# Two experts in one tile: slots of 64 rows, half-width matmuls, the second half's weights copied by ScalarE

## The chip, the cores and the metric

The kernel runs on one core of one Trainium2 chip. The metric is device time in microseconds (us) of one execution, the median of several.

## What is computed

A transformer block in fp32: causal attention with 16 heads on 4 x 512 tokens of width 512, between layer norms, and then a mixture of experts. Only the second part matters here. Each of 2048 tokens goes to 8 of 64 experts, each a gated layer of width 128, and the 8 results are added with their weights. A shared expert is added for every token.

```python
E = 64; K = 8; D = 512; F = 128; FS = 128
logits = xt @ router_w.T
probs = jax.nn.softmax(logits.astype(jnp.float32), axis=-1)
top_w, top_i = jax.lax.top_k(probs, K)
top_w = top_w / jnp.sum(top_w, axis=-1, keepdims=True)
comb = comb.at[jnp.arange(T)[:, None], top_i].set(top_w)
def step(acc, ws):
    wg_e, wu_e, wd_e, we = ws
    h = jax.nn.silu(xt @ wg_e.T) * (xt @ wu_e.T) @ wd_e.T
    return (acc + we[:, None] * h, None)
routed, _ = jax.lax.scan(step, jnp.zeros_like(xt), (Wg, Wu, Wd, comb.T))
```

## The kernel before

The program of each engine is written out by hand, with semaphores between them. After attention (to about 430 us) and the router, VectorE (DVE) and TensorE (PE) sort the 2048 x 8 pairs of token and expert by expert into slots; each expert's rows are padded to a multiple of 128, so a tile of 128 slots belongs to one expert. `place_rows` and `tile_rows` (PE) and lines L1180 to L1252 (DVE) work out the first slot of each expert (`below`, `steps`), the expert of each tile (`col_i`), the slot of the ring in which its weights lie (`ring_i`), the number of expert weights that a tile needs loaded (`weights_i`), the tile after which a ring slot is free (`ends_i`) and the number of loop bodies (`pairs_i`). The table of tokens, 128 rows by `HIGH` = 192 tiles, is filled by 128 pairs of one-hot matrices (DVE, L1243 and L1244) and matmuls (PE, L910), beside the shared expert's 16 tiles (L853, L863, L869).

Then the expert loop runs over 6q + 1 tiles in bodies of six (`DEEP`). For a tile t:

- GpSimd (POOL) gathers 128 rows of activations and router weights by index (L458), up to six tiles ahead, and after `down` adds 128 result rows to one of three sum tables in memory (L464). It is the only engine that issues these.
- PE: `turn_rows` transposes the rows (L940, four of 128x128), `up` multiplies them with the gate and up weights (L956, four matmuls of 256 moving columns), `turn_hidden` transposes the gated product (L962) and `down` multiplies it with the down weights (L967, one of 512 columns). In the loop the order is `down(t-1)`, `turn_rows(t+2)`, `turn_hidden(t)`, `up(t+1)`.
- ScalarE (ACT): `silu(t)` (L659), then `turned(t+2)`, which waits that the weights of the tile are loaded (`s_ready`, the index from `weights_i`, L651) and copies the turned rows out of PSUM (L654).
- DVE: `hide(t)` (L1277), `take_y(t-1)` (L1284, L1285), `take_hidden(t)` (L1289), `weight(t+1)` (L1271, one column of the gathered row, found by a register load from `col_i`) and `stage_gather` (L1262).
- SyncE (SP) loads each expert's 768 KB into a ring of eight (L353) when the last tile that uses the slot is through (`s_dn`).

In attention, `weigh` (L779) multiplies with 32 columns of weights into four groups of 32 PSUM partitions, and `score` (L729) uses 32 rows in four groups. After the loop three tables are added, normalised and written out.

## Time and profile before

| | us |
|---|---|
| median of 3 runs | 1173.48 (1173.42 to 1176.66) |
| profiled execution | 1176.2 |
| its span, first to last instruction | 1174.3 |
| PE busy | 1080.3 |
| DVE busy | 683.6 |
| POOL busy | 630.4 |
| ACT busy | 483.4 |

The span is divided by engine. PE is busy nearly all the time; the other engines are busy for about half of it. Busy time tells how much work an engine has, not who waits: for that the groups of instructions, the waits and the order of time in a short stretch are read. Times in rows are us, durations of one instruction ns where so marked. A group "x1264" counts records; an fp32 matmul has two. POOL's `DMA_INDIRECT` is the time in which it writes out a gather or scatter, not that of the transfer.

### The profile page before, as it was taken

The page shows a single profiled execution, that of the slowest core. Times are in us where ns is not written, and L with a number is a line of the kernel's source. Part 1 is how long each engine was busy: PE and PEld are TensorE (multiplying, and loading weights), DVE is VectorE, ACT ScalarE, POOL GpSimd, SP SyncE. Part 2 cuts the span into 40 slices and gives each one's busy share as a digit, 9 for nine tenths or more (in the row PEclk, how much of TensorE's full clock was granted, in tenths as well). Part 3 has the DMA queues.
Part 4 walks back from the last instruction along what each step waited for, and adds up shares of the span by engine and source line. Part 5 has one row for each costly group of instructions (what it writes and reads, how often), then busy time and mean ns, then how long its engine had stood idle before and what let it go on. Part 6 is the DMA issues. An engine that isn't in the chain of part 4 may idle for free.

```text
span 1174.3 us, 24363 instructions
## 1 busy us (share of the span) xinstructions
PE 1080.3 (92%) x6281; PEld 726.1 (62%) x6282; DVE 683.6 (58%) x2349; ACT 483.4 (41%) x1357; POOL 630.4 (54%) x648
## 2 busy tenths in 40 slices
PE   6999899999999979988879999999999999999973
PEld 3555566555656546555547777777777777767631
DVE  5666566556666668868845444455444444545447
ACT  2666566656666644433212222222222222222223
POOL 3533333333333313321148788888888888888724
PEclk9999999999999999989979999999999999999987
DMA  8700000000000042100259999999999999997796
GB/s 315 287 2 1 3 1 1 2 2 1 1 2 2 1 187 91 63 19 19 72 177 212 222 198 252 248 234 240 260 232 250 243 229 277 272 226 148 110 334 240
DMA packets 66279, 166.71 MB, mean 142 GB/s; under 512 B 15379, under 2 KB 17171, under 8 KB 66081
## 3 DMA queue, kind: packets, MB, share of 16 engines
q0 software_dynamic: 38496, 83.95, 32.6%
q1 hardware_dynamic: 27712, 81.88, 19.7%
q8 instruction: 38, 0.62, 0.2%
q14 instruction: 33, 0.26, 0.1%
HBM read 119.85 MB, written 62.65 MB: 155 GB/s over the span
## 4 chain that ended last, share of the span: by engine, by line
PE 71%; DMA 12%; DVE 6%; issue 4%; ACT 2%; POOL 2%; POOLq 0%; DVEq 0%; SPq 0%; ACTq 0%
PE ps L956 15%; PE ps L700 15%; DMA sum_rows<-x_t,idx 8%; PE ps L967 8%; PE ps L759 6%; PE ps L817 4%; PE ps L729 4%; PE ps L940 4%; PE ps L779 4%; DMA x_t<-x_rows,idx 3%; PE ps L853 3%; PE ps L714 2%; PE ps L869 1%; PE ps L833 1%; POOL x_t L458 1%
## 5 line engine op out<-in xcount | busy, mean ns | idle before, releaser
L956 PE MATMUL ps<-big,work 128*128 x1264 | 300.5, 381 | 0.0
L464 POOL DMA_INDIRECT sum_rows<-x_t,idx x157 | 250.0, 1592 | 52.3 <-issue 40.2
L956 PEld LDWEIGHTS ps<-big,work 128*128 128x128 f32 x1264 | 229.0, 191 | 24.9
L458 POOL DMA_INDIRECT x_t<-x_rows,idx x159 | 166.2, 1045 | 63.5 <-issue 28.1
L700 PE MATMUL ps<-big 128*128 128x384 f32 x512 | 181.5, 499 | 2.1 <-ACT big L533 1.7
L384 POOL TENSOR_TENSOR work<-qkv_all,rope_sb 128x256 f32<-128x256 f32 x64 | 46.7, 729 | 245.2 <-ACT qkv_all L538 245.2
L654 ACT ACTIVATE work<-ps 128x512 f32<-128x512 f32 x159 | 95.0, 597 | 192.6 <-PE ps L940 131.6
L967 PE MATMUL ps<-big,work 128*128 x314 | 161.2, 595 | 1.8 <-issue 1.6
L940 PEld LDWEIGHTS ps<-ident_sb,x_t 128*128 128x128 f32 x636 | 78.7, 142 | 101.6 <-issue 71.0
L1061 DVE CUSTOM_DVE_ANT_0 ps<-ps,mask_sb 128x128 f32<-128x128 f32 (+3 forms) x256 | 120.6, 512 | 23.8 <-PE ps L729 23.0
L557 ACT ACTIVATE work<-ps,neg_max 128x128 f32<-128x128 f32 (+3 forms) x256 | 132.5, 528 | 3.3 <-DVE neg_max L1061 2.4
L700 PEld LDWEIGHTS ps<-big 128*128 128x128 f32 x512 | 94.8, 195 | 57.3 <-issue 4.6
L1277 DVE SCALAR_TENSOR_TENSOR work<-work,small,ps 128x128 f32<-128x128 f32 x157 | 54.5, 347 | 124.7 <-ACT work L659 97.1
L659 ACT ACTIVATE work<-ps 128x128 f32<-128x128 f32 x157 | 43.6, 278 | 196.4 <-PE ps L956 145.6
L563 ACT ACTIVATE x_t<-ps 128x128 f32<-128x128 f32 (+2 forms) x192 | 77.0, 436 | 90.6 <-PE ps L759 90.6
L940 PE MATMUL ps<-ident_sb,x_t 128*128 128x128 f32 x636 | 97.3, 276 | 14.2 <-DMA x_t<-x_rows,idx 12.5
L759 PE MATMUL ps<-ident_sb,work 128*128 128x128 f32 x640 | 98.5, 284 | 9.7 <-issue 6.6
L1285 DVE TENSOR_SCALAR x_t<-ps 128x512 f32<-128x512 f32 x157 | 106.9, 681 | 0.0
L759 PEld LDWEIGHTS ps<-ident_sb,work 128*128 128x128 f32 x640 | 68.8, 141 | 46.7 <-issue 35.7
L1082 DVE TENSOR_TENSOR attn_t<-ps,work 128x128 f32 (+1 forms) x64 | 18.7, 292 | 111.0 <-PE ps L779 111.0
L1271 DVE TENSOR_SCALAR small<-x_t 128x1 f32 x158 | 24.3, 154 | 76.1 <-issue 72.3
L967 PEld LDWEIGHTS ps<-big,work 128*128 128x128 f32 x314 | 58.9, 190 | 12.9 <-issue 5.2
(177 smaller groups left out, 1459.9 us busy)
## 6 DMA issues: line engine op xcount, KB each, us to landing
big<-experts SPq DMA_DIRECT2D x65, 768.0 KB, 14.5
sum_rows<-x_t POOLq DMA_DIRECT2D x4, 2048.0 KB
big<-sum_rows SPq DMA_DIRECT2D x8, 768.0 KB, 9.5
x_rows<-work SPq DMA_DIRECT2D x16, 256.0 KB, 2.0
sum_rows<-attn_t POOLq DMA_DIRECT2D x2, 2048.0 KB
out<-x_sb SPq DMA_DIRECT2D x16, 256.0 KB, 5.2
x_sb<-x SPq DMA_DIRECT2D x3, 1024.0 KB, 10.2
x_t<-sum_rows SPq DMA_DIRECT2D x4, 768.0 KB, 13.1
```

Of the source, the lines that this page charges most:

```text
L458: pool.indirect_dma_start(rows[:, q, :], None, x2_rows, bass.IndirectOffsetOnAxis(ap=idx[:, q, 0:1], axis=0), bounds_check=last_row, oob_i ...
L464: pool.indirect_dma_start(all_sums, bass.IndirectOffsetOnAxis(ap=idx[:, q, 1:2], axis=0), y_sb[:, q, :], None, bounds_check=last_sum, oob_ ...
L557: act.activation(probs[:, h, 0:n], s_bank[h][:, 0:n], ACT.Exp, bias=neg_max[:, h:h + 1], scale=-1.0, accum_out=den[:, h:h + 1]).then_inc(s ...
L563: act.activation(probs_t[:, i % 2, h, 0:qt + 1, :], pt_bank[h % 2].rearrange("p (k n) -> p k n", k=TB)[:, 0:qt + 1, :], ACT.Copy).then_inc ...
L654: act.activation(rows_t[:, p, :, :], ps[:, p, :].rearrange("p (c n) -> p c n", c=DC), ACT.Copy).then_inc(s_xg, 1)
L700: mm = pe.matmul(bank[:, 0:QKV], x_t[:, c, bass.ts(t, P)], wqkv_sb[:, c, g % G, :], start=(c == 0), stop=(c == DC - 1))
L759: mm = pe.transpose(pt_bank[h % 2][:, bass.ts(c, P)], probs[:, h, bass.ts(c, P)], ident_sb[:, :])
L940: mm = pe.transpose(ps[:, p, bass.ts(c, P)], rows[:, q, bass.ts(c, P)], ident_sb[:, :])
L956: mm = pe.matmul(ps[:, 2 + p, 0:GATEUP], rows_t[:, p, c, :], w_ring[:, slot, c * GATEUP:(c + 1) * GATEUP], start=(c == 0), stop=(c == DC - 1))
L967: pe.matmul(ps[:, 5 + p, :], hidden_t[:, p, :], w_ring[:, slot, DC * GATEUP:WCOLS], start=True, stop=True).then_inc(s_dn, 1)
L1061: dve.tensor_tensor_reduce(sc, sc, mask_sb[:, S - n:S], -SCALE, 3.0e38, ALU.add, ALU.min, neg_max[:, h:h + 1]).then_inc(s_masked, 1)
L1285: dve.tensor_scalar(y_sb[:, q, :], ps[:, 5 + q % 2, :], 1.0, None, ALU.mult).then_inc(s_y, 1)
```

## The change

Slots are counted in units of `GRAIN` = 64: each expert's rows are padded to a multiple of 64, and a tile of 128 slots has two halves that may belong to two experts. `HIGH` becomes 162. `up` and `down` are issued as two matmuls each, one per half: 64 columns of weights (the activations) into PSUM partitions 0 to 63 or 64 to 127. The moving operand of the first half is read from the ring at an address from a register, that of the second from a fixed place, `wb_up` and `wb_down` (two buffers each, in what was attention's `qkv_all`). ACT copies it there for every tile, `copy_up` 128x1024 and `copy_down` 128x512, also where both halves have the same expert. The row's weight is picked by a comparison of the 64 router weights with the half's expert (`expert_p`) and a sum. The tables are worked out for both halves. Left out below are declarations.

```diff
@@ -31,9 +31,12 @@
 NW = 8
 XROW = D + E
-HIGH = (B * S * K + E * (P - 1)) // P + 1
+GRAIN = 64
+PARTS = P // GRAIN
+PART_BITS = PARTS.bit_length() - 1
+DEEP = 6
+HIGH = -(-((B * S * K + E * (GRAIN - 1)) // GRAIN + 1) // (PARTS * DEEP)) * DEEP
 RING = 8
-DEEP = 6
 TABLES = 3
 COLS = HIGH + 2 * DEEP
...
+        wb_up = qkv_all[:, 0:2 * DC * GATEUP].rearrange("p (a n) -> p a n", a=2)
+        wb_down = qkv_all[:, 2 * DC * GATEUP:2 * WCOLS].rearrange("p (a n) -> p a n", a=2)
+        picked = work[:, 2432:2432 + E]
...
+        def tile_expert(q):
+            return ps[0:1, 7, 96:96 + HIGH] if q == 0 else ps[0:1, 6, (q - 1) * HIGH:q * HIGH]
...
-                    end = sp.value_load(ends_i[0:1, bass.ts(j * NW + r, 1)], min_val=1, max_val=HIGH)
+                    end = sp.value_load(ends_i[0:1, bass.ts(j * NW + r, 1)], min_val=1, max_val=HIGH + 1)
...
+            pool.wait_ge(s_wb_up, full * DEEP + (DEEP + 3))
+            pool.sem_inc(s_issue, 1)
+            pool.wait_ge(s_wb_down, full * DEEP + (DEEP + 2))
+            pool.sem_inc(s_issue, 1)
...
-            def turned(t, p):
+            b_slots = [act.alloc_register(f"b_slot{k}") for k in range(DEEP + 1)]
+
+            def load_b(first):
+
+                act.load(b_slots, slot_b[0:1, bass.ds(first, DEEP + 1)])
+
+            def b_slot_of(k):
+                return act.snap(b_slots[k], min_val=0, max_val=NW - 1)
+
+            def copy_up(t, p, slot):
 
                 need = act.value_load(weights_i[0:1, bass.ts(t, 1)], min_val=1, max_val=E)
                 act.wait_ge(s_ready, need)
+                if not isinstance(t, int) or t >= 2:
+                    act.wait_ge(s_gu, t - 1)
+                act.activation(wb_up[:, p, :], w_ring[:, slot, 0:DC * GATEUP], ACT.Copy).then_inc(s_wb_up, 1)
+
+            def copy_down(t, p, slot):
+
+                if not isinstance(t, int) or t >= 2:
+                    act.wait_ge(s_dn, t)
+                act.activation(wb_down[:, p, :], w_ring[:, slot, DC * GATEUP:WCOLS], ACT.Copy).then_inc(s_wb_down, 1)
+
+            def turned(t, p):
+
                 act.wait_ge(s_xg_ps, t + 1)
                 act.activation(rows_t[:, p, :, :], ps[:, p, :].rearrange("p (c n) -> p c n", c=DC),
                                ACT.Copy).then_inc(s_xg, 1)
                 act.wait_ge(s_gu, t + 1)
                 act.activation(gate[:, p, :], ps[:, 2 + p, 0:F], ACT.Silu).then_inc(s_gate, 1)
 
+            act.wait_ge(s_table, 1)
+            act.load(b_slots[0:3], slot_b[0:1, 0:3])
+            copy_up(0, 0, b_slot_of(0))
             turned(0, 0)
+            copy_down(0, 0, b_slot_of(0))
+            copy_up(1, 1, b_slot_of(1))
             turned(1, 1)
             silu(0, 0)
+            copy_up(2, 0, b_slot_of(2))
+            copy_down(1, 1, b_slot_of(1))
             turned(2, 0)
             with act.Fori(0, quads) as j:
+                load_b(j * DEEP + 2)
                 for c in range(DEEP):
                     t = j * DEEP + (c + 1)
-                    silu(t, (c + 1) % 2)
-                    turned(t + 2, (c + 1) % 2)
+                    p = (c + 1) % 2
+                    silu(t, p)
+                    copy_up(t + 2, p, b_slot_of(c + 1))
+                    copy_down(t + 1, 1 - p, b_slot_of(c))
+                    turned(t + 2, p)
             act.preload_act_table(ACT.Sqrt)
             for i in range(TILES + 1):
                 if i < TILES:
...
 
             def tile_rows():
-                pe.wait_ge(s_cnt, 2)
-                pe.matmul(tables[0:1, 96:96 + HIGH], ones_sb[0:E, 0:1], past_end, start=True, stop=True).then_inc(s_row_ps, 1)
+                pe.wait_ge(s_cnt, 1 + PARTS)
+                for q in range(PARTS):
+                    pe.matmul(tables[GRAIN * q:GRAIN * (q + 1), 96:96 + HIGH], ones_sb[0:E - 1, 0:GRAIN], past_end[0:E - 1, q, :],
+                              start=True, stop=True)
+                for q in range(1, PARTS):
+                    mm = pe.matmul(tile_expert(q), ones_sb[0:E - 1, 0:1], past_end[0:E - 1, q, :], start=True, stop=True)
+                mm.then_inc(s_row_ps, 1)
 
             def fill_table(n):
 
...
 
                 pe.wait_ge(s_xg, t + 1)
+                pe.wait_ge(s_wb_up, t + 1)
                 for c in range(DC):
-                    mm = pe.matmul(ps[:, 2 + p, 0:GATEUP], rows_t[:, p, c, :], w_ring[:, slot, c * GATEUP:(c + 1) * GATEUP],
+                    pe.matmul(ps[0:GRAIN, 2 + p, 0:GATEUP], rows_t[:, p, c, 0:GRAIN], w_ring[:, slot, c * GATEUP:(c + 1) * GATEUP],
+                              start=(c == 0), stop=(c == DC - 1))
+                    mm = pe.matmul(ps[GRAIN:P, 2 + p, 0:GATEUP], rows_t[:, p, c, GRAIN:P], wb_up[:, p, c * GATEUP:(c + 1) * GATEUP],
                                    start=(c == 0), stop=(c == DC - 1))
                 mm.then_inc(s_gu, 1)
 
...
 
                 pe.wait_ge(s_ht, t + 1)
-                pe.matmul(ps[:, 5 + p, :], hidden_t[:, p, :], w_ring[:, slot, DC * GATEUP:WCOLS],
+                pe.wait_ge(s_wb_down, t + 1)
+                pe.matmul(ps[0:GRAIN, 5 + p, :], hidden_t[:, p, 0:GRAIN], w_ring[:, slot, DC * GATEUP:WCOLS], start=True, stop=True)
+                pe.matmul(ps[GRAIN:P, 5 + p, :], hidden_t[:, p, GRAIN:P], wb_down[:, p, :],
                           start=True, stop=True).then_inc(s_dn, 1)
 
             pe.wait_ge(s_table, 1)
...
-            dve.tensor_copy(n_col[:, 2:3], ps[0:E, 7, 8:9]).then_inc(s_own, 1)
-            dve.tensor_scalar(ends_i[:, :], ps[0:1, 7, 16:16 + E], 1.0, None, ALU.add).then_inc(s_tables, 1)
-            own[0] += 1
+            for q in range(PARTS):
+                dve.tensor_scalar(n_col[:, 2 + q:3 + q], ps[0:E, 7, 8:9], float(q), None, ALU.subtract).then_inc(s_own, 1)
+            dve.tensor_scalar(ends_i[:, :], ps[0:1, 7, 16:16 + E], float(2 * PARTS - 1), None, ALU.add).then_inc(s_own, 1)
+            own[0] += 1 + PARTS
+            dve.wait_ge(s_own, own[0])
+            dve.tensor_scalar(ends_i[:, :], ends_i[:, :], PART_BITS, None, ALU.logical_shift_right).then_inc(s_tables, 1)
-            step(dve.tensor_scalar(bodies, ps[0:1, 7, 15 + E:16 + E], (DEEP - 3) / 2, 1.0 / DEEP, ALU.add, ALU.mult))
+            step(dve.tensor_scalar(bodies, ps[0:1, 7, 15 + E:16 + E], PARTS * (DEEP / 2 - 1) - 0.5, 1.0 / (DEEP * PARTS), ALU.add, ALU.mult))
-            dve.tensor_scalar(past_end, count_sb[0:E, :], n_col[:, 2:3], None, ALU.is_ge).then_inc(s_cnt, 1)
+            for q in range(PARTS):
+                dve.tensor_scalar(past_end[:, q, :], count_sb[0:E, :], float(PARTS), n_col[:, 2 + q:3 + q], ALU.mult,
+                                  ALU.is_ge).then_inc(s_cnt, 1)
...
-            tile_expert = ps[0:1, 7, 96:96 + HIGH]
-            dve.memset(col_i[:, HIGH:COLS], E - 1).then_inc(s_own, 1)
-            dve.memset(weights_i[:, HIGH:COLS], E).then_inc(s_own, 1)
-            own[0] += 2
-            step(dve.tensor_scalar(col_i[:, 0:HIGH], tile_expert, float(E - 1), None, ALU.min))
-            dve.tensor_scalar(weights_i[:, 0:HIGH], tile_expert, float(E - 1), 1.0, ALU.min, ALU.add).then_inc(s_tables, 1)
-            by_body = col_i[:, :].rearrange("o (j k) -> o j k", k=DEEP)
+            dve.memset(col_i[:, :, HIGH:COLS], E - 1).then_inc(s_own, 1)
+            dve.memset(expert_p[:, HIGH:COLS], E - 1).then_inc(s_own, 1)
+            dve.tensor_copy(expert_p[:, 0:HIGH], ps[:, 7, 96:96 + HIGH]).then_inc(s_own, 1)
+            for q in range(PARTS):
+                dve.tensor_copy(col_i[:, q, 0:HIGH], tile_expert(q)).then_inc(s_own, 1)
+            own[0] += 3 + PARTS
+            dve.wait_ge(s_own, own[0])
+            dve.tensor_scalar(weights_i[:, :], col_i[:, 1, :], 1, None, ALU.add).then_inc(s_own, 1)
+            dve.tensor_scalar(slot_b[:, :], col_i[:, 1, :], NW - 1, None, ALU.bitwise_and).then_inc(s_tables, 1)
+            own[0] += 1
+            by_body = col_i[:, 0, :].rearrange("o (j k) -> o j k", k=DEEP)
...
 
-            def expert_of(t):
-                return dve.value_load(col_i[0:1, bass.ts(t, 1)], min_val=0, max_val=E - 1)
-
             def weight(t, q, r):
 
-                col = expert_of(t)
                 dve.wait_ge(s_gather[q], r)
-                dve.tensor_scalar(wcol[:, q % 2:q % 2 + 1], rows[:, q, D:XROW][:, bass.ts(col, 1)], 1.0, None,
-                                  ALU.mult).then_inc(s_weight, 1)
+                dve.scalar_tensor_tensor(out=picked[:, :], in0=count_sb[:, 0:E], scalar=expert_p[:, bass.ts(t, 1)],
+                                         in1=rows[:, q, D:XROW], op0=ALU.is_equal, op1=ALU.mult,
+                                         accum_out=wcol[:, q % 2:q % 2 + 1]).then_inc(s_weight, 1)
 
             def hide(t, p):
                 dve.wait_ge(s_gate, t + 1)
...
-        "below": P * (e[:, None] < e[None, :]),
-        "steps": np.broadcast_to(P * np.arange(TILES), (E, TILES)),
+        "below": GRAIN * (e[:, None] < e[None, :]),
+        "steps": np.broadcast_to(GRAIN * np.arange(B * S // GRAIN), (E, B * S // GRAIN)),
```

## Rows read from the trace of the kernel before

**Rows 1.** The page: busy us by engine; shares of the chain that ended last.
```profile
PE 1080.3 (92%) x6281; PEld 726.1 (62%) x6282; DVE 683.6 (58%) x2349; ACT 483.4 (41%) x1357; POOL 630.4 (54%) x648
...
PE 71%; DMA 12%; DVE 6%; issue 4%; ACT 2%; POOL 2%; POOLq 0%; DVEq 0%; SPq 0%; ACTq 0%
```

**Rows 2.** Groups of instructions, PE: count of records, busy us, mean ns, idle before.
```profile
L967 PE MATMUL ps<-big,work 128*128 x314 | 161.2, 595 | 1.8 <-issue 1.6
```

**Rows 3.** Order of time: start us, us, instruction; `down` of tiles 0, 12 and 156.
```profile
609.04 0.59 PE L967 MATMUL ps<-big,work 128*128 x1
...
646.64 0.59 PE L967 MATMUL ps<-big,work 128*128 x1
...
1112.13 1.12 PE L967 MATMUL ps<-big,work 128*128 x2
```

**Rows 4.** Stretches: us, busy PE, PEld, DVE, ACT, POOL, clock, DMA share, GB/s.
```profile
609.00:646.60 37.60, 37.60 (x181) 28.82 (x181) 19.01 (x72) 10.50 (x24) 29.00 (x22) 1.00 0.81 188
646.60:1112.10 465.50, 456.27 (x2161) 343.30 (x2160) 229.12 (x864) 127.10 (x289) 376.87 (x285) 1.00 0.94 228
```

**Rows 5.** Order of time, PE, one tile of the loop.
```profile
764.11 1.89 PE L956 MATMUL ps<-big,work 128*128 x8
765.84 1.02 PE L967 MATMUL ps<-big,work 128*128 x2
766.70 0.60 PE L940 MATMUL ps<-ident_sb,x_t 128*128 128x128 f32 x4
```

**Rows 6.** Order of time, POOL, two scatters.
```profile
762.28 1.59 POOL L464 DMA_INDIRECT sum_rows<-x_t,idx  x1 [0.30 <-issue]
...
765.53 1.59 POOL L464 DMA_INDIRECT sum_rows<-x_t,idx  x1 [0.31 <-issue]
```

**Rows 7.** Order of time: POOL's gathers of tiles 12 and 156.
```profile
627.13 1.05 POOL L458 DMA_INDIRECT x_t<-x_rows,idx  x1 [0.30 <-DVE x_t L1285]
...
1096.70 1.05 POOL L458 DMA_INDIRECT x_t<-x_rows,idx  x1 [0.30 <-issue]
```

**Rows 8.** Waits in the loop: engine, line, releaser, total us, times, longest.
```profile
PEld ps L940 <- DMA x_t<-x_rows,idx: 22.2, 29, 2.0
```

**Rows 9.** Order of time, PE, attention: `weigh` in four column groups, 307.95 on.
```profile
307.95 1.08 PE L779 MATMUL ps<-x_t,qkv_all 128*32 128x128 f32 x32
```

**Rows 10.** Order of time, PE, cut close: from full width into column groups.
```profile
301.36 0.49 PE L700 MATMUL ps<-big 128*128 128x384 f32 x1
301.77 0.32 PE L779 MATMUL ps<-x_t,qkv_all 128*32 128x128 f32 x4
```

**Rows 11.** The same, from full width into row groups of 32.
```profile
200.87 0.27 PE L714 MATMUL ps<-ident_sb,work 128*128 128x128 f32 x1
201.07 0.39 PE L729 MATMUL ps<-big 32*128 32x128 f32 x4
```

**Rows 12.** The same, out of column groups.
```profile
302.23 0.40 PE L779 MATMUL ps<-x_t,qkv_all 128*32 128x128 f32 x8
302.56 0.33 PE L759 MATMUL ps<-ident_sb,work 128*128 128x128 f32 x1
```

**Rows 13.** Single lines, ACT and its queue: ns min/median/max, first and last start.
```profile
L628 ACT ACTIVATE wo_sb<-wo_sb x1: 1056/1056/1056, 511.6 to 511.6; 128x1024 f32<-128x1024 f32 x1
...
L654 ACT ACTIVATE work<-ps x159: 597/597/598, 601.7 to 1110.4; 128x512 f32<-128x512 f32 x159
...
L651 ACTq FUSED_REGOPS  x315: 42/147/162, 585.0 to 1109.8; - x158
L651 ACTq TENSOR_LOAD <-weights_i x159: 273/286/1080, 584.1 to 1109.1; - x159
```

**Rows 14.** Order of time, DVE, behind the shared expert.
```profile
586.19 0.32 DVE L1244 TENSOR_SCALAR high<-count_h,work,token_sb 128x192 f16<-128x192 f16 x1
586.43 0.24 DVE L1243 TENSOR_SCALAR low<-count_h,work 128x128 f16<-128x128 f16 x1
```

**Rows 15.** Order of time, PE, within the shared expert.
```profile
546.30 0.82 PE L910 MATMUL ps<-high,low 128*128 128x192 f16 x8
```

16 lines of the change are left out of this document (10 added, 6 removed).

## The prediction, made before the change was run

> **What bounds the kernel now.** I read the page from the top, then only the stage that the change touches. The first lines [rows 1] show TensorE (PE) busy for 92% of the span and as 71% of the chain that ended last, but also 12% of that chain on DMAs. That mixture asks for the second step, the stretch of the expert loop.
>
> The groups of instructions [rows 2] give the number of tiles. One fp32 matmul is recorded as two, so 314 of L967 (`down`, one matmul per tile) are 157 tiles. The first `down` starts at 609.04, the last pair at 1112.13 [rows 3]: 503.1 us for 156 steps, 3.225 us a tile.
>
> Two paces make this mean. The 13th `down` starts at 646.64 [rows 3], so the first 12 steps took 37.6 us, 3.133 each, and there PE was busy 37.60 of 37.60 us [rows 4]. One tile in such a stretch [rows 5] shows why: `up` starts at 764.11, `down` at 765.84, the row turns at 766.70, four with 0.109 from start to start (0.60 less the 0.27 of the last, by three); with the hidden turn, another 0.11, the next `up` is due at 767.24. That is 3.13 us without a gap, PE's own pace. Beside it, GpSimd (POOL) alternates a scatter of 1.59 and a gather of 1.05 us [rows 7], each 0.30 behind the one before, and its scatters start at 762.28 and 765.53 [rows 6]: 3.25 us a tile, slower than PE. From the 13th gather (627.13) to the 157th (1096.70) it is 469.6/144 = 3.261. So PE runs on the lead of six gathers and is then held to POOL's pace; its weight loads waited 22.2 us for gathers [rows 8]. ACT and DVE wait most of the time. The DMA engines are 94% busy [rows 4], so a third limit is near too.
>
> **The change part by part.**
>
> *Fewer tiles.* Padding each expert's rows to 64 instead of 128 changes the count of tiles. Running the reference's routing on its inputs gives rows per expert; rounding each to 128 gives 156 tiles, to 64 gives 290 half tiles, 145 tiles. The loop runs 6q+1 tiles: 157 before (as the trace has), 145 after (q = 24; a 291st half would make it 151). Only 37 of the 145 hold two experts. At an unchanged pace 12 tiles are 12 x 3.225 = 38.7 us. This is all that can be won in the loop, and the rest of the sum is what it costs.
>
> *Matmuls in half width.* `up` goes from 4 matmuls of 128 columns of weights to 8 of 64, `down` from 1 to 2. A step of `up` lasts 0.216 us per instruction (eight from 764.11 to 765.84), one of `down` 0.43 (765.84 to 766.70, two) [rows 5]. One after the other the halves would add 8 x 0.216 + 2 x 0.43 = 2.59 us a tile. The trace has the same form in attention: L779 writes four column groups of 32. There 32 instructions took 1.08 us [rows 9]; minus the 0.27 that one lasts, 31 starts in 0.81, 26 ns each, where a full-width instruction of the same 128 columns starts every 109 ns (the row turns above). Four column groups run at the same time, so I take two groups of 64 to do so too, at no added streaming time.
>
> *Change of array shape.* Each tile now goes from full-width turns into `up` in column groups, and out of `down` back to full-width turns: one entry and one exit. Both are in attention. Entry [rows 10]: the last L700 starts at 301.36 and streams 384 columns, three times 0.109; L779 starts at 301.77, 0.08 to 0.09 late. The first four of L779 span 0.32 where 0.02 + 0.27 would do: 0.02 to 0.03 more. Together 0.117 with 32 columns of weights. With row groups and 128 columns [rows 11], the last L714 starts at 200.87, a step is 0.11, L729 starts at 201.07: 0.09 late, and its four span 0.39 instead of 0.29: 0.10 more, together 0.198. For 64 columns I interpolate a third of the way: 0.144. Exit [rows 12]: eight of L779 span 302.23 to 302.63, so the last starts at 302.36 and streams to 302.47; L759 starts at 302.56 and lasts 0.33 where 0.27 is normal: 0.15. Sum 0.29 a tile; bounds 0.24 and 0.35, and, as a floor, 0 (switch hidden).
>
> So PE's own pace is 3.133 + 0.294 = 3.427 us, above POOL's 3.261, which per tile is unchanged. The waits for gathers go, since a PE slower than POOL keeps the lead of six gathers, as in the first 12 steps. What comes late next is PE itself. The stretch is 144 x 3.427 = 493.5 us against 503.1: -9.6 us.
>
> *Copies by ScalarE.* `copy_up` moves 128x1024 and `copy_down` 128x512 in every tile. L628, 128x1024 from SBUF to SBUF, took 1.056 us; L654, 128x512, takes 0.597 [rows 13]. ACT gets 1.65 us a tile on top of 127.10/144 = 0.88 [rows 4]. The load of the needed index (0.286) and its register steps stand between `silu` and the next activation, 0.48 us by their rows (0.286, 0.042, 0.147) [rows 13] and 0.70 with what I allow for a check and the gaps. The copies need two more waits and the slot's address, at most 0.35 more (two steps of 0.147 and their gaps). ACT's round is then at most 0.70 + 0.35 + 1.06 + 0.60 + 0.60 = 3.31, and with a load of seven slots once in six tiles (PE's own such load hides in its queue; ACT's may not; 0.08) 3.39, less where one activation overlaps the next: I take 3.1 to 3.4, hidden under PE's 3.427, but with little cover. `copy_up(t+2)` and `copy_down(t+1)` are queued behind `silu(t)` and ahead of `turned(t+2)`; `silu(t+1)` stands behind all of them, and on it wait `hide`, the hidden turn and `up`. Their results are needed by PE one tile later, so the new waits of PE on `s_wb_up` and `s_wb_down` cost nothing as long as ACT's round is below PE's.
>
> *VectorE.* The weight of a row becomes a 128x64 compare-multiply with a sum instead of a 128x1 copy. The nearest row, a two-step 128x192, took 0.32 [rows 14]; DVE is busy 229 of 465 us [rows 4], half of a tile, and a register load goes. Nothing.
>
> *GpSimd, SyncE, weights.* The same instructions per tile, 12 tiles fewer; two more waits after the loop, long fulfilled. Expert loads are the same 56. Rows moved are the same 16384 each way.
>
> *Tables.* 162 columns instead of 192. Behind the shared expert 30-odd pairs of L1243/L1244 go at DVE's pace, and L1243 starts 0.24 behind L1244 [rows 14]: 1.25 ns for each of 192 columns, 0.037 for 30, 32 pairs -1.2 us. In the 12 shared tiles PE sets the pace; L910 there starts every 0.08, 0.66 for eight [rows 15], and 30/192 of it is 0.10: -1.2. The new small DVE and PE operations (about ten of 0.15 to 0.35, most in place of others) add 0.3 to 2, mostly absorbed by DVE's waits in the shared tiles: +0.6. Sum -1.8 (between -3 and 0).
>
> *Start of the loop.* Five copies stand in ACT's first instructions. The first is done before the first rows land; `copy_up(2)` and `copy_down(1)` put `turned(2)` behind 1.65 us and with it `silu(1)`: +1.0 (0 to 2.5).
>
> **Sum**: -9.6 - 1.8 + 1.0 = -10.4. The profiled execution took 1176.2 (span 1174.3, 1.9 around it), 2.7 above the median of 1173.48; the change is taken from the median: 1163.1 us, ratio 0.991.
>
> **The rivals.**
>
> *ACT's round is the bound (0.13).* If each copy costs more than its row (a dynamic address, two semaphores, a drained queue ahead of the load), say 0.1 for each of two, the round is 3.6. For: the cover is 0.04 to 0.3 only. Against: activations overlap. It decides from a round of 3.43, and beats the 12 saved tiles from 3.49. Price: 144 x (3.6 - 3.427) = +24.9: 1188.
>
> *The halves don't run together (0.08).* An fp32 matmul is two passes. If PE holds passes to program order, A1 A2 B1 B2, the second half starts only with A2: one `down` step of 0.43 more a tile, +62: 1225 (0.05). Fully serial is +2.59 x 144 = 372: 1535 (0.03). Against: four matmuls in two passes kept to order would need 17 steps of 109 ns for 32 instructions, 1.85 us, and took 0.81 [rows 9].
> The Trainium skill, page "TensorE: Matmul & The Clock Gate", section on packing small matmuls, says that matmuls start and end in strict program order. By it the passes would be staggered and the time would be 1225; rows 9 disagree, or the passes are not in that order.
>
> *The switches are hidden (0.08).* Then POOL stays the bound: 144 x 3.261 = 469.6, -33.5 in the loop: 1139. Against: each entry and exit in rows 10 to 12 shows its gap.
>
> *Transfers are the bound (0.08).* The engines are 94% busy over 465.5 us and 81% over 37.6 [rows 4], 468 us of work that doesn't shrink. In 493.5 they would be 95% busy. If that queueing holds the loop at 503: 1173.
>
> *151 tiles (0.03).* A row count just over a multiple of 64 by another rounding: 6 x 3.427 more, 1184.
>
> **How the numbers follow.** The forecast has 0.60, with its own range 1156 (0.24 a tile, tables -3) to 1172 (0.35). The range of 8 in 10 leaves out the hidden switches, the serial halves and the worst third of ACT's case: 1150 to 1186. A difference under 0.3% (3.5 us) can't be told from none. Faster than 1170: 0.57 of the forecast, 0.08, and 0.01 of the transfers, 0.66. Within: 0.03 + 0.06 + 0.02 of ACT's, 0.11. Slower than 1177: 0.23.
>
> **What would show it.** 580 records of `down` (145 tiles, two halves, two passes); `down` to `down` 3.4 us without waits for gathers, and POOL now waiting for PE; a gap of about 0.1 at the first `up` and of 0.15 at the first row turn; ACT's round below 3.43 with some idle time left before `silu`. It would be wrong if the gap at the switches is over 0.36 a tile, if PE waits for `wb_up` or ACT's `silu`, or if matmuls in pairs start further apart than 0.216.

## The result, and the profile after

The changed kernel takes 1180.26 us (median of 6 runs, 1179.58 to 1181.62) beside 1174.20 of the kernel before (6 runs, 1172.83 to 1176.66): ratio 1.0041, 95% interval 1.0029 to 1.0052. It is 0.4% slower, where 1163.1 was forecast. Run once more in the third set below it took 1180.97 us, ratio 1.0044 (1.0027 to 1.0061).

The page of the changed kernel, whose profiled execution took 1181.62 (span 1179.8): busy us by engine, shares of the chain that ended last, and the groups that answer to [rows 1, 2].

```profile
PE 1093.3 (93%) x7563; PEld 623.9 (53%) x7564; DVE 657.7 (56%) x2428; ACT 687.4 (58%) x1626; POOL 596.8 (51%) x624
PE 87%; DVE 6%; issue 2%; ACT 2%; DMA 2%; DVEq 0%; SPq 0%; POOL 0%; ACTq 0%; POOLq 0%
...
L1013 PE MATMUL ps<-qkv_all,work 128*64 128x256 f32 x1168 | 285.1, 387 | 0.0
L1011 PE MATMUL ps<-big,work 128*64 x1168 | 284.8, 387 | 0.0
L477 POOL DMA_INDIRECT sum_rows<-x_t,idx x145 | 230.6, 1590 | 94.6 <-issue 44.1
L681 ACT ACTIVATE qkv_all<-big 128x1024 f32 x147 | 155.4, 1057 | 90.4 <-issue 88.3
L1025 PE MATMUL ps<-big,work 128*64 x290 | 149.2, 596 | 2.0 <-issue 1.5
L994 PE MATMUL ps<-ident_sb,x_t 128*128 128x128 f32 x588 | 97.6, 289 | 6.6 <-DMA x_t<-x_rows,idx 6.6
```

The DMAs have all but gone from the chain (12% to 2%), PE holds 87% of it, and POOL sits idle 94.6 us before its scatters, where it was 52.3 before: the bound has moved from POOL to PE, as forecast. L1025 has 290 records, 145 tiles. Order of time, the first and the last `down` (L1025 first half, L1026 second), which answer to [rows 3]:

```profile
608.75 0.59 PE L1025 MATMUL ps<-big,work 128*64 x1
...
1117.86 0.64 PE L1025 MATMUL ps<-big,work 128*64 x1
```

The same stretch as one row, which answers to [rows 4] (us, busy PE, PEld, DVE, ACT, POOL, clock, DMA share, GB/s):

```profile
608.70:1117.90 509.20, 506.13 (x3605) 271.40 (x3600) 221.08 (x1008) 337.11 (x578) 374.26 (x284) 1.00 0.91 222
```

PE has its full clock, and the DMAs are less busy than before (0.91). The loop takes 509.1 us against 503.1, 6.0 more. The part ahead of it is 0.3 shorter and the part behind 0.2. So the whole difference lies in the loop, and there 144 steps have a mean of 3.536 us. Their median is 3.44 and their minimum 3.43, where 3.427 was forecast. One tile of the median kind, order of time on PE, answers to [rows 5]:

```profile
761.03 0.59 PE L1025 MATMUL ps<-big,work 128*64 x1
761.04 0.59 PE L1026 MATMUL ps<-qkv_all,work 128*64 128x512 f32 x1
761.46 0.59 PE L1025 MATMUL ps<-big,work 128*64 x1
761.47 0.59 PE L1026 MATMUL ps<-qkv_all,work 128*64 128x512 f32 x1
761.99 0.66 PE L994 MATMUL ps<-ident_sb,x_t 128*128 128x128 f32 x4
762.48 0.27 PE L1019 MATMUL ps<-ident_sb,work 128*128 128x128 f32 x1
762.68 0.43 PE L1011 MATMUL ps<-big,work 128*64 x1
762.69 0.43 PE L1013 MATMUL ps<-qkv_all,work 128*64 128x256 f32 x1
762.95 0.38 PE L1011 MATMUL ps<-big,work 128*64 x1
...
764.46 0.59 PE L1025 MATMUL ps<-big,work 128*64 x1
```

The two halves start 0.01 apart and a step of `up` is still 0.216: they run together at no streaming cost. The exit from column groups shows as 761.46 to 761.99, 0.53 where a full-width `down` has 0.43. The entry shows as 762.48 to 762.68, 0.20 where 0.11 was, and a first step of 0.27 instead of 0.216. With the slower first of the four turns that makes 3.43. The price of the switches was right. What is not forecast is that the mean lies 0.10 us above the median. Sorted by place in the loop's body of six tiles, the steps are 3.50, 3.43, 3.58, 3.46, 3.45 and 3.79: the excess sits mostly in the third and the last.

In those two, `silu` is late. Order of time on ACT, with its idle time ahead of `silu` (L697) and its releaser in brackets:

```profile
761.25 0.28 ACT L697 ACTIVATE work<-ps 128x128 f32<-128x128 f32 x1 [0.72 <-PE ps L1013]
762.05 1.06 ACT L681 ACTIVATE qkv_all<-big 128x1024 f32 x1 [0.52 <-issue]
763.01 0.61 ACT L687 ACTIVATE qkv_all<-big 128x512 f32 x1
763.53 0.58 ACT L692 ACTIVATE work<-ps 128x512 f32<-128x512 f32 x1
765.26 0.28 ACT L697 ACTIVATE work<-ps 128x128 f32<-128x128 f32 x1 [1.15 <-PE ps L1013]
...
768.26 0.28 ACT L697 ACTIVATE work<-ps 128x128 f32<-128x128 f32 x1 [0.15 <-PE ps L1013]
...
775.68 0.28 ACT L697 ACTIVATE work<-ps 128x128 f32<-128x128 f32 x1 [1.14 <-PE ps L1013]
...
779.10 0.28 ACT L697 ACTIVATE work<-ps 128x128 f32<-128x128 f32 x1 [0.58 <-issue]
```

`silu` at 761.25 is 0.22 behind the start of `down` (761.03); at 765.26 it is 0.80 behind (764.46). ACT had finished `turned` at 764.11 and sat idle for 1.15 us: it was not busy, it waited for `up`'s signal, the semaphore update that its last matmul makes. By the semaphore events of the trace that signal came 0.40 us behind the start of the last `up` matmul in most tiles and 0.95 to 1.0 in two of six. (The trace lacks the events of some tiles; more on that below.) VectorE's product follows `silu`, and the hidden turn (L1019) and `up` follow that:

```profile
765.42 0.66 PE L994 MATMUL ps<-ident_sb,x_t 128*128 128x128 f32 x4
765.97 0.33 PE L1019 MATMUL ps<-ident_sb,work 128*128 128x128 f32 x1
766.27 0.42 PE L1011 MATMUL ps<-big,work 128*64 x1
...
768.04 0.59 PE L1025 MATMUL ps<-big,work 128*64 x1
```

The turn starts 0.55 behind L994 instead of 0.49, `up` 0.30 behind the turn instead of 0.20, and the step is 3.58. From 765.26 to the next `silu` it is 3.00 us: that is ACT's round when it waits 0.15 us only. After 775.68 it is 3.42, and the load of seven slots stands in between (a single line of ACT's queue, ns min/median/max):

```profile
L670 ACTq TENSOR_LOAD <-slot_b x24: 979/1450/2309, 607.1 to 1095.6; - x24
```

So I had two suspects for the 14.7 us above 144 x 3.433: the load of seven (theory A), and something in half-width pairs themselves (rival B).

### The profile page after: what moved, and what is told of

It reads as the page before. It is cut to its first block, busy times and chain, and to the rows that moved or that the text cites. A ratio compares the mean times of both kernels' runs of the same rounds, so it can differ in the third digit from the quotient of the medians.

```text
span 1179.8 us, 27207 instructions
## 1 busy us (share of the span) xinstructions
PE 1093.3 (93%) x7563; PEld 623.9 (53%) x7564; DVE 657.7 (56%) x2428; ACT 687.4 (58%) x1626; POOL 596.8 (51%) x624
## 4 chain that ended last, share of the span: by engine, by line
PE 87%; DVE 6%; issue 2%; ACT 2%; DMA 2%; DVEq 0%; SPq 0%; POOL 0%; ACTq 0%; POOLq 0%
PE ps L1011 23%; PE ps L749 15%; PE ps L1025 11%; PE ps L994 7%; PE ps L808 6%; PE ps L866 4%; PE ps L778 4%; PE ps L828 4%; PE ps L902 3%; PE ps L1019 2%; PE ps L763 2%; PE ps L918 1%; PE ps L882 1%; PE ps L1013 1%; DVE stats L1390 1%
## 5 line engine op out<-in xcount | busy, mean ns | idle before, releaser
L1013 PE MATMUL ps<-qkv_all,work 128*64 128x256 f32 x1168 | 285.1, 387 | 0.0
L1011 PE MATMUL ps<-big,work 128*64 x1168 | 284.8, 387 | 0.0
L477 POOL DMA_INDIRECT sum_rows<-x_t,idx x145 | 230.6, 1590 | 94.6 <-issue 44.1
L681 ACT ACTIVATE qkv_all<-big 128x1024 f32 x147 | 155.4, 1057 | 90.4 <-issue 88.3
L1011 PEld LDWEIGHTS ps<-big,work 128*64 128x64 f32 x1168 | 148.6, 137 | 86.6 <-issue 25.2
L471 POOL DMA_INDIRECT x_t<-x_rows,idx x147 | 153.3, 1043 | 59.4 <-issue 42.1
L1025 PE MATMUL ps<-big,work 128*64 x290 | 149.2, 596 | 2.0 <-issue 1.5
L1026 PE MATMUL ps<-qkv_all,work 128*64 128x512 f32 x290 | 149.3, 596 | 0.0
L1013 PEld LDWEIGHTS ps<-qkv_all,work 128*64 128x64 f32 x1168 | 148.6, 137 | 0.0
L994 PEld LDWEIGHTS ps<-ident_sb,x_t 128*128 128x128 f32 x588 | 62.4, 142 | 124.8 <-issue 117.6
L994 PE MATMUL ps<-ident_sb,x_t 128*128 128x128 f32 x588 | 97.6, 289 | 6.6 <-DMA x_t<-x_rows,idx 6.6
L1350 DVE TENSOR_SCALAR x_t<-ps 128x512 f32<-128x512 f32 x145 | 98.7, 680 | 0.0
L697 ACT ACTIVATE work<-ps 128x128 f32<-128x128 f32 x145 | 40.2, 277 | 97.7 <-PE ps L1013 90.8
```

What stands on the lines that cost most here:

```text
L471: pool.indirect_dma_start(rows[:, q, :], None, x2_rows, bass.IndirectOffsetOnAxis(ap=idx[:, q, 0:1], axis=0), bounds_check=last_row, oob_i ...
L477: pool.indirect_dma_start(all_sums, bass.IndirectOffsetOnAxis(ap=idx[:, q, 1:2], axis=0), y_sb[:, q, :], None, bounds_check=last_sum, oob_ ...
L681: act.activation(wb_up[:, p, :], w_ring[:, slot, 0:DC * GATEUP], ACT.Copy).then_inc(s_wb_up, 1)
L994: mm = pe.transpose(ps[:, p, bass.ts(c, P)], rows[:, q, bass.ts(c, P)], ident_sb[:, :])
L1011: pe.matmul(ps[0:GRAIN, 2 + p, 0:GATEUP], rows_t[:, p, c, 0:GRAIN], w_ring[:, slot, c * GATEUP:(c + 1) * GATEUP], start=(c == 0), stop=(c ...
L1013: mm = pe.matmul(ps[GRAIN:P, 2 + p, 0:GATEUP], rows_t[:, p, c, GRAIN:P], wb_up[:, p, c * GATEUP:(c + 1) * GATEUP], start=(c == 0), stop=(c ...
```

## The experiments

Eighteen runs were made in five sets, each set on one chip beside the kernel before. "Loop" is the time from the first `down` to the last.

| run | set | us | ratio, 95% interval | loop us |
|---|---|---|---|---|
| full width, no copies: e1, e15 | 1, 4 | 1139.5, 1137.8 | 0.9689, 0.9688 (both within 0.965 to 0.973) | 467.6, 468.4 |
| full width, copies: e3, e16 | 1, 4 | 1139.3, 1139.2 | 0.9702, 0.9703 (0.968 to 0.973) | 468.8, 468.7 |
| half width, no copies: e2 | 1 | 1169.7 | 0.9957 (0.9940 to 0.9973) | 497.8 |
| the same, e7 and e11 | 2, 3 | 1175.5, 1173.1 | 0.9990 (0.9974 to 1.0005), 0.9982 (0.9972 to 0.9991) | 503.3, 503.3 |
| one slot a tile: e4 | 1 | 1171.1 | 0.9971 (0.9957 to 0.9985) | 500.3 |
| the same, e6 and e10 | 2, 3 | 1183.8, 1184.0 | 1.0065 (1.0049 to 1.0082), 1.0065 (1.0041 to 1.0090) | 513.6, 512.7 |
| list loaded later: e8 | 2 | 1180.7 | 1.0040 (1.0030 to 1.0051) | 509.1 |
| changed kernel: e9 | 3 | 1181.0 | 1.0044 (1.0027 to 1.0061) | 509.1 |
| marks: e14 | 4 | 1173.2 | 0.9984 (0.9967 to 1.0001) | 502.8 |
| fixed weights: e18 | 5 | 1166.5 | 0.9923 (0.9898 to 0.9949) | 496.0 |
| pairs: e5, e12 | 2, 3 | 1434.9, 1286.4 | 1.219, 1.094 | 760.3, 611.7 |
| pairs: e13 | 4 | 1171.5 | 0.9969 (0.9951 to 0.9988) | 492.1 |
| pairs: e17 | 5 | 1166.2 | 0.9927 (0.9908 to 0.9946) | 487.0 |

### Half width and copies, one without the other

```diff
 e1, e3 (down likewise)
-    pe.matmul(ps[0:GRAIN, 2 + p, ...], rows_t[:, p, c, 0:GRAIN], w_ring[:, slot, ...])
-    mm = pe.matmul(ps[GRAIN:P, 2 + p, ...], rows_t[:, p, c, GRAIN:P], wb_up[:, p, ...])
+    mm = pe.matmul(ps[:, 2 + p, ...], rows_t[:, p, c, :], w_ring[:, slot, ...])
 e1, e2
-    act.activation(wb_up[:, p, :], w_ring[:, slot, 0:DC * GATEUP], ACT.Copy).then_inc(s_wb_up, 1)
-    act.activation(wb_down[:, p, :], w_ring[:, slot, DC * GATEUP:WCOLS], ACT.Copy).then_inc(s_wb_down, 1)
-    load_b(j * DEEP + 2)
-    pe.wait_ge(s_wb_up, t + 1)
-    pe.wait_ge(s_wb_down, t + 1)
```

> The changed kernel with 145 tiles, but each tile's products are again full-width (128 columns, the first half's expert for all 128 rows) and ScalarE copies nothing and loads no list of slots. The second half's rows get the wrong expert's weights, so that part of the computation is left out. It prices the fewer tiles and the new tables alone. Both theories expect the same: PE's own pace is back at 3.133 us, so POOL's 3.261 us a tile sets the stretch: 144 x 3.27 = 471 us in place of 509, the kernel at 1138 to 1148 us. Above 1155 would say that the tables or the fewer tiles cost something that the forecast did not price.

> The changed kernel with its half-width pairs of matmuls, but without ScalarE's two copies, its list of slots and the waits for them; the second half reads what the fixed place happens to hold, so the second expert's part is left out. Theory A (ScalarE's round is what lifts the mean from 3.44 to 3.54 us a tile: late silu and the load of seven registers once per six tiles): every tile falls back to the median, 144 x 3.44 = 495 us, the kernel at 1166 us (1163 to 1169), silu starts 0.4 us after the last up matmul in every tile. Rival B (the half-width pairs themselves make the signal behind the up pass late in every third tile): two tiles in six keep a silu that starts about 1.0 us after the last up matmul, mean 3.49 or more, 1172 to 1178 us.

> The changed kernel with ScalarE's copies, its list and their waits as they are, but with full-width matmuls that use the first half's expert alone (the second expert's part is left out). Theory A: PE needs 3.133 us, POOL 3.261, and ScalarE's round with the list sets the pace where it is longer: mean 3.32 to 3.42 us a tile, 478 to 492 us, the kernel at 1149 to 1163 us. Rival B (half-width pairs are the cause, ScalarE is covered): POOL's 3.27, 1138 to 1148 us, as without the copies.

e1 gives the fewer tiles and the new tables alone: 1139.5 us, a mean step of 3.25 us with POOL as the bound, so the 12 tiles were worth 35 us. e3 adds the copies and the list, and it costs nothing (468.8 against 467.6). This speaks against theory A: ACT's round with copies is no longer than the 3.26 us of its mean step. e2 adds half width in place of copies: +30.2 us of loop. Its median step is 3.433 where e1 has 3.133, so the two switches cost 0.300 us a tile; 0.294 was forecast. In e2 no signal of the loop was late, and `silu` stood 0.43 us behind the last `up` matmul.

e2's 497.8 is still 3.4 above 144 x 3.433. That lies at the end of the body of six, means of 3.54 and 3.47 in place of 3.43. Order of time on PE there, and the load of eight ring slots in PE's queue, of e2:

```profile
836.26 0.38 PE L999 MATMUL ps<-big,work 128*64 x1
836.26 0.38 PE L1001 MATMUL ps<-qkv_all,work 128*64 128x256 f32 x1
836.64 0.64 PE L1012 MATMUL ps<-big,work 128*64 x1
...
837.12 0.59 PE L1012 MATMUL ps<-big,work 128*64 x1
...
L990 PEldq TENSOR_LOAD <-ring_i x25: 591/1127/1317, 599.5 to 1104.8; - x25
```

`down` starts 0.38 behind the last `up` where 0.21 is a step, and its second pass 0.48 behind where 0.43 is one. The length of this load decides. In e2 it takes 0.59 to 1.32 us in the loop, and wherever it exceeds 1.0 (but for the last, ahead of the loop's exit), `down` starts 0.65 to 0.68 us behind its end and the step is longer than 3.43. It is no matter of half width. In the kernel before, the first 12 steps have two loop ends among them and stand at 3.133 throughout, but the loads there took 0.6 us. Eight of its 26 loads at a loop end took 1.04 to 1.37 us, and behind those `down` started 0.35 to 0.77 us after the last `up` matmul instead of 0.22. One of them, in order of time, where `down` was due at 762.40, and the line of all loads:

```profile
760.67 1.89 PE L956 MATMUL ps<-big,work 128*128 x8
...
762.61 1.12 PE L967 MATMUL ps<-big,work 128*128 x2
...
L947 PEldq TENSOR_LOAD <-ring_i x27: 587/604/1372, 600.5 to 1110.5; - x27
```

What differs is how often the load is long: its median is 0.60 us in the kernel before, 0.59 in e1 and 1.13 in e2. Why, no run shows.

### The list of seven slots

```diff
 e4: second_i holds, for each tile, what to wait for and the slot
-    load_b(j * DEEP + 2)             # seven registers once in six tiles
+    act.load([second[p]], second_i[0:1, bass.ts(t, 1), 1:2])   # one a tile
 e6: e4, and once in six tiles
+    act.load(spare, second_i[0:1, bass.ds(j * DEEP + 2, DEEP + 1), 1:2])
 e7: e2 with load_b(j * DEEP + 2) back
 e8: the changed kernel, load_b moved behind the body's last copy_down
```

> The whole changed computation; only ScalarE's load of seven slots once per six tiles is replaced by a load of one slot per tile beside the one that is there. Theory A: the long tile at the end of each body of six (3.788 us against 3.44) goes, 24 x 0.35 = 8 us, and the added load of about 0.3 us lies in ScalarE's slack of 0.1 us or less, so part is given back: mean 3.46 to 3.52 us, 1169 to 1177 us. Rival B (the list has nothing to do with it): ScalarE's round only grows by the added load, mean 3.54 to 3.75, 1181 to 1210 us.

> The run with one slot a tile, plus a load of seven words into registers that nobody reads, once per six tiles at the place where the changed kernel loads its list. Theory A (the load as such, 1.0 to 1.9 us in which ScalarE starts nothing, is what costs): at least the 8 us come back, 1178 to 1186 us, and silu is late in some tiles of each body again. Rival C (the load is harmless; what cost was the use of the list's registers or the order of ScalarE's instructions): 1170 to 1174 us.

> Half-width matmuls without the copies (the second expert's part is left out), but with ScalarE's load of seven slots once per six tiles. Theory A (the load costs only because ScalarE has no slack beside the copies): 1168 to 1172 us and silu 0.43 us after the last up matmul in every tile but perhaps the body's first. Rival B2 (load and half-width matmuls are enough for the late signal): silu is 0.9 to 1.0 us late in two tiles of six and the kernel takes 1172 to 1177 us.

> The changed kernel with the load of seven slots moved from ahead of the body's first silu to behind the last copy of the body before, ahead of the copy of turned rows, which TensorE reads a whole tile later. Theory A1 (the load costs by holding silu): most of the 11 us goes, 1170 to 1174 us. Theory A2 (ScalarE's round is full, wherever the load stands it spills over into the next tiles): 1177 to 1182 us, with silu late in the tiles after it.

e4 gave 1171.1 us, no late signal in any tile, and a loop of 500.3: by theory A, as it seemed. Then e6 gave 1183.8 and e7 1175.5, as if the load were the cause. It was not. In e6 and e7 nobody reads the loaded registers, and the load was dropped when the kernels were built. The trace of e6 has no such record and as many instructions as e4's (27470), and e7's as many as e2's (26014). e6 is e4 and e7 is e2, on another chip, 12.7 and 5.8 us slower, while the kernel before differed by 1.4 (1175.7 against 1174.2). e8 leaves the list and moves it, and nothing changes (509.1 us of loop, as in the changed kernel).

> The changed kernel itself, unaltered, beside the next two runs on one chip. Two pairs of runs that differ in no instruction (half-width without copies: 1169.7 and 1175.5 us; one slot a tile: 1171.1 and 1183.8 us) came out apart on two chips, so the chip has to be held fixed. Theory P (a late signal behind the up pass is a matter of the chip, not of ScalarE's list): on a chip with late signals this is at 1178 to 1182 us and the two others are as slow as they were on the second chip; on a chip without them it is at 1170 to 1174 us. Theory A (the list of seven is the cause): 1178 to 1182 us on any chip.

> One slot a tile, as before, on the same chip as the changed kernel of this set. Theory P: within 4 us of the changed kernel, either both near 1171 or both at 1180 to 1184 us. Theory A: 8 to 11 us faster than the changed kernel.

> Half-width pairs without the copies (the second expert's part is left out), on the same chip. Theory P: 1168 to 1171 us where signals are in time (ScalarE's copies then cost under 3 us beside it), 1172 to 1178 us where they are late (the copies then cost 5 to 8 us more). Theory A: 1168 to 1171 us on any chip.

All three on one chip: 1181.0 for the changed kernel, 1184.0 with one slot a tile, 1173.1 without copies. Theory A had wanted e10 8 to 11 us faster than e9; it is 3 us slower, with `silu` late in four tiles of six instead of two. So the list of seven is not what makes e9 slower than e4, and my reading of e4 was wrong. What differs is whether the signal behind `up` is late. e2 and e11 are one kernel. Order of time, `down`'s start and `silu` of the same tile, first e2, then e11, and below each, from the view of `silu`'s line, ACT's idle time before it that PE's `up` ended (us, times):

```profile
822.74 0.59 PE L1012 MATMUL ps<-big,work 128*64 x1
822.96 0.28 ACT L688 ACTIVATE work<-ps 128x128 f32<-128x128 f32 x1 [1.40 <-PE ps L1001]
...
  PE ps L1001: 204.6, 145
```

```profile
824.99 0.59 PE L1012 MATMUL ps<-big,work 128*64 x1
825.76 0.28 ACT L688 ACTIVATE work<-ps 128x128 f32<-128x128 f32 x1 [1.95 <-PE ps L1001]
...
  PE ps L1001: 220.2, 134
```

ACT has nothing to copy in either and waits for PE, 1.40 us in one and 1.95 in the other (in total 204.6 and 220.2 us, and in e11 another 16.7 without a releaser on record). Within such a tile the matmuls stand the same in both. On this footing the terms can be read off: late signals cost 503.3 - 497.8 = 5.5 us with ACT unloaded. The copies and their list cost 509.1 - 503.3 = 5.8 more where signals are late, and 500.3 - 497.8 = 2.5 with one slot a tile where they are not. The 5.5 compares two chips, and it is the lateness together with what it drags along: in e11 PE's loads of eight slots are shorter than in e2 (median 0.76 us against 1.13), and still `down` follows 0.65 to 0.71 behind the end of most of them.

One more thing differs between the sets, and it leaves a rival that nothing here rules out. The traces of set 1 hold an event for every signal of `up`; those of the other sets lack part of their events on every engine (e11 has 9238 in all, e2, the same kernel, 12197). In the changed kernel's trace the signals of 26 tiles are missing, nearly all of them of the tile right behind a place where signals come late. So the late signals may belong to the recording of the trace on those chips rather than to the kernel. No run was made without the recording, so none can tell.

### What is late: the matmuls or the signal

```diff
 e14: e2 with a semaphore behind every up matmul
+    pe.matmul(ps[0:GRAIN, ...], ..., w_ring[...]).then_inc(s_mark1, 1)
+    mm.then_inc(s_mark2 if c < DC - 1 else s_gu, 1)
 e18: e2 with both halves reading wb_up and wb_down, no address from a register
```

> Half-width pairs without the copies (the second expert's part is left out), with a semaphore that nobody waits for raised behind every up matmul of either half. The trace then shows when each of the eight matmuls of a tile ends. Theory L1 (the second half really lags in some tiles): its marks fall behind those of the first half before the last one, by up to 0.57 us. Theory L2 (only the signal of the last matmul is held back): all marks but the last stand 0.21 to 0.44 us apart as in other tiles, and the last comes 0.5 us late in two tiles of six. Theory L3 (the signal is held where few semaphore updates are made): with the marks the lateness goes. The time itself should be 1169 to 1178 us.

> Full-width matmuls with the first half's expert alone, no copies (the second expert's part is left out), on the chip of this set. POOL's 3.26 us a tile sets the pace: 1137 to 1142 us, and the signal behind the up pass comes 0.39 us after the last matmul in every tile, whatever the half-width kernels show on the same chip.

> Full-width matmuls with the first half's expert alone, with ScalarE's copies and its list (the second expert's part is left out). If the copies cost only where signals are late, and full width has none late: within 2 us of the run without them, 1137 to 1142 us. If ScalarE's round is full by itself on this chip: 1145 to 1155 us.

> Half-width pairs without the copies, both halves reading the fixed place, none the ring (no expert's weights are used: that part of the computation is left out), so no matmul of the expert passes has an address from a register. If the late signal belongs to register-addressed operands of the one half beside fixed ones of the other, silu is 0.43 us behind the last up matmul in every tile and the time 1167 to 1171 us; if it belongs to half-width pairs whatever they read, silu stays 0.9 to 1.0 us behind in two tiles of six, on a chip that shows it, and the time is 1171 to 1177 us.

Semaphore events of e14, in us from the start of a tile's `up`, whose last matmul starts at 1.57; the trace lacks some events, the first of each half among them:

```
tile   first half         second half   s_gu   down's signal
65     1.09 1.52 1.95     1.13 1.57     2.00   2.83
66     1.09      2.44          1.74     2.48   2.83
69     1.09 1.75 2.50     1.13 2.46     2.54   2.83
```

None of the three theories holds as written. It is not one half that lags (L1) and not the last signal alone (L2): from the third matmul on, the signals of both halves are 0.2 and then 0.5 us late (in tile 69 one is 0.9). More updates don't cure it (L3). `down`'s signal is on time in these tiles, though its matmuls follow the late ones on the same engine, so I take the signals to be held, not the work; by what, the runs don't say. e15, on the same chip, has all its signals 0.39 to 0.45 us behind the matmul. e16, full width with copies, has eight of 115 in the loop at 0.5 to 0.9, in no fixed place of the body, and both have the times of e1 and e3: at full width the lateness is rare and no cost of it shows. e18 still has late signals, by 0.39 to 0.47 us in two tiles of six, so addresses from registers are not the cause, though they may add to it. It also has no slots to load, and its loop ends cost 0.04 us in place of 0.14, with late signals present. That confirms the load of eight slots as the price of the loop end in e2: 496.0 is only 1.6 above 144 x 3.433.

### Half the switches

The change of shape is the largest price, 0.300 x 144 = 43 us. So I let PE take two tiles together: eight row turns, two hidden turns, two `up`, two `down`.

```diff
 PE, e5
-    down(t - 1); turn_rows(t + 2); turn_hidden(t); up(t + 1)
+    turn_rows(e + 4); turn_rows(e + 5); turn_hidden(e); turn_hidden(e + 1)
+    up(e + 2); up(e + 3); down(e); down(e + 1)
 POOL, e12: gather(t + 8) ahead of scatter(t - 1), not gather(t + 6)
 ACT, e13
-    silu; copy_up; turned
+    silu; turned; copy_up
 DVE, e17
-    hide(e + 2); hide(e + 3); take_y(e); take_y(e + 1)
+    hide(e + 2); take_y(e); hide(e + 3); take_y(e + 1)
```

> The whole computation, built on the run with one slot a tile: TensorE takes two tiles together, four turned row blocks twice, both hidden transposes, then both up passes and both down passes, so the array changes between full and half width once per two tiles in place of once per tile; ScalarE's and VectorE's orders are regrouped to fit. Theory: the change of shape costs 0.30 us a time (3.133 to 3.433 us a tile), so a pair needs 2 x 3.433 - 0.30 = 6.566 us, 3.283 a tile, just above POOL's 3.261; 144 x 3.30 = 475 us in place of 500, the kernel at 1146 us (1141 to 1153). Rival: the 0.30 us is not the change of shape but belongs to half-width blocks as such (each block's first and last matmul), or the gathers and ScalarE's round become late in the new order: 1160 to 1175 us.

> The whole computation, two tiles together on TensorE as in the run at 1435 us, but GpSimd sends the gather of each tile two tiles earlier, so that it no longer stands behind the two scatters of the pair before. Theory: the 1435 us was a loop of y, two scatters and two gathers of 10 us per pair; with it open, a pair needs 2 x 3.433 - 0.30 = 6.57 us on TensorE against 6.52 on GpSimd: 3.28 to 3.33 us a tile, 1143 to 1153 us. Rival: the loop only moves to another wait (VectorE's copy of y or the weight of the next rows) and it stays over 1200 us.

> The whole computation, two tiles together on TensorE and early gathers as in the run at 1286 us, with ScalarE's copy of the turned rows moved ahead of the copy of the up weights. Theory: the 1286 us was a loop through ScalarE (up pass, silu, copy of weights, turned rows, next turn into the same bank: 7.5 us a pair); with turned rows ahead of the weights it closes in about 5 us, and a pair needs 2 x 3.433 - 0.30 = 6.57 us on TensorE or, where the signal behind the up pass is 0.57 us late, up to 6.8: 3.28 to 3.40 us a tile, 1143 to 1160 us. Rival: the weights are now what is late (ScalarE's round of two tiles is fuller than 6.6 us): 1165 to 1250 us.

> The whole computation, pairs as in the run at 1171 us, with VectorE's copy of the first y of a pair moved ahead of the product for the second tile of the next pair, so GpSimd gets its first scatter 0.7 us earlier and the second 0.4 us earlier in each pair of 6.6 us. In the run before, 32 of 72 pairs took the 6.56 us that TensorE needs and the rest up to 8.4. Theory: the longer pairs wait for GpSimd's burst and its transfers, and get shorter by up to 0.5 us each: 36 x 0.3 to 0.5 us, 1153 to 1163 us. Rival: they wait for ScalarE or for transfers that are full anyway: 1168 to 1174 us.

Twice a loop through another engine took the gain, and the waits named it. In e5 the gather for the next pair stood behind the scatters of the last; in e12 the turn into a bank waited for ACT's copy out of it. Waits in the loop (us in total, times, longest), first e5, then e12:

```profile
PE ps L992 <- DMA x_t<-x_rows,idx: 178.5, 57, 6.5
```

```profile
PE ps L992 <- ACT work L689: 98.3, 70, 2.4
```

Part of these two times is clock: with PE busy for 558.6 of 760 us e5 was granted 0.85 over its loop, and e12 0.96, where e17 has 1.00. e13 opens the second loop too. Of its 72 steps from pair to pair 31 take 6.56 us, against 6.566 worked out (2 x 3.433 - 0.30); the rest take up to 8.4. In e17, with VectorE's order changed, 38 are at 6.56, and the loop is 487.0. Its stretch as one row:

```profile
613.00:1100.00 487.00, 474.13 (x3563) 274.24 (x3559) 220.48 (x1000) 326.33 (x574) 371.18 (x282) 1.00 0.94 231
```

e17 takes 1166.2 us, 0.7% less than the kernel before and 14 us less than the changed one. A pair takes 6.76 us on average there, within 4% of what PE and POOL each need (6.56 and 6.52), so I take each wait of one to be lost to the other; no run tests it. The sets differ, so e17 against e13 (5 us) holds both the edit and the chip; the loops, 487.0 against 492.1, say the same.

## Why the prediction was wrong

**The bound now, tiles, halves together, switches.** Right. 157 to 145 tiles, POOL's pace in e1, halves 0.01 apart, 0.300 against 0.294 for the switches, median step 3.44 against 3.427. The waits for gathers, 22.2 us in the loop [rows 8], are gone: PE's 6.6 us before L994 all lie ahead of the first `down`. The staggered halves (1225) are out, since the halves start 0.01 apart in each pass. The Trainium skill, page "TensorE: Matmul & The Clock Gate", section "Part 3: Packing small matmuls", says that matmuls start and end in strict program order. The rows agree with that only if the passes of the two halves alternate in the program, which no trace tells. The rival "transfers" is out as well: DMAs are 2% of the chain.

**The step that failed: "The stretch is 144 x 3.427 = 493.5".** It took PE's pace in a clean tile for the mean of all tiles. Measured is 509.1, 15.6 more. The pace itself is 0.9 of it (144 x 3.433 is 494.4). The rest is three terms that the prediction put at nothing: PE's load of eight slots at the loop's end +3.4 (e2, confirmed by e18); late signals +5.5 (e11 against e2, two chips); the copies with the list +5.8 beside late signals (e9 against e11). The terms act together, so on one chip they needn't split in this way. The load could have been seen: the prediction says that "PE's own such load hides in its queue", a reading of 12 steps in which it took 0.6 us. In the same trace eight of 26 such loads took over 1.0 us, and `down` came late behind them; the mean there was POOL's pace and didn't show it. The late signals are in no row of the kernel before, and their cause is open.

**"Copies by ScalarE".** The durations were right (1.06 and 0.61 us against 1.056 and 0.597). The sum of the round was not: 0.70 + 0.35 + 1.06 + 0.60 + 0.60 leaves out `silu`'s own 0.28, and with it the upper bound is 3.59, above PE's pace. The round came out shorter all the same, 3.00 us from `silu` to `silu` at 765.26, since 0.52 us stand behind `silu` where 1.05 was allowed and the activations overlap by 0.1. It was 3.42 where the list stands in between. With full width the copies are hidden (e3); with half width and signals in time they cost 2.5 us of loop (e4 against e2). The warning "hidden but with little cover" was right: with 0.57 us of lateness against 0.43 of cover (PE's 3.43 less ACT's 3.00), the next `silu` is late too. I had priced the rival "ACT's round is the bound" at 1188; what came is neither it nor the forecast, a round that is short enough on average and late in two tiles of six.

**Tables and start of the loop.** -0.8 was forecast (-1.8 and +1.0), -0.3 came ahead of the first `down`. Both are small. I didn't take them apart.

**The range** held the time (1150 to 1186), but the direction was wrong, and that it held is in good part luck: its room above 1172 was left for a slow round of ACT, not for late signals and loads. The forecast's own range ended at 1172 (its lower end, by its own terms, is 1154 and not 1156), and its terms for the unknown were about the size of the switches and the tables, none about the difference between the median and the mean of a loop.

## What to carry to other kernels

A loop that goes from one bound to another must be costed by its mean with all that the old bound had hidden: a load in the sequencer, a signal that comes late, the end of the body. Here 0.10 us a tile of such things were more than the 0.06 that was left after the switches (494.4 us against 503.1, over 144 steps). A change between full-width and column-group matmuls cost 0.15 us each time, so matmuls of one shape belong together; grouping two tiles halved it, but only after the orders of three other engines had been fitted to it. That a thing is hidden must be read from all its occurrences, not from the first stretch: the load at the loop's end was hidden in 12 steps and not in all of the rest. And an experiment that seems to confirm a theory on one chip must be run beside its control on that same chip: e4 alone would have blamed a list that is not the cause.

## What the runs showed of the hardware

- A kernel of half-width matmul pairs had PE's signals 0.4 to 0.6 us late in two tiles of six on four of the five chips of these sets (sets 2 to 5; in set 5 0.39 to 0.47; with one slot a tile `silu` was late in four) and none late in the loop on one (set 1); the same instructions took 1171.1 and 1183.8 us. Full-width kernels had none in the loop in e1, e3 and e15, and eight of 115 in e16. The traces with late signals all lack events, so the recording may have a part in it. The cause is open.
- Two matmuls in column groups of 64 that read different operands ran together, 7 ns apart (median). Each fp32 matmul left two records, and they came in the order first half, second half, first half, second half, though the kernel's text has the whole matmul of the first half ahead of the other.
- Loads of several registers took 1.0 to 2.3 us on ACT (seven words) and 0.6 to 1.4 on PE's queue (eight), where one word took 0.29 (median) on ACT. `down` started no less than 0.65 us behind the end of the load ahead of it, in the kernel before, e1 and e2 alike, but for the load at the loop's exit; loads over about 0.85 us (full width) or 1.0 us (e2) showed in PE's time.
